# Two small round trips through DRAM are moved from SyncE's queue to GpSimd's, and the first groups are reordered

## The reference

```
x = x + rg_lru(layernorm(x))                      # a gated recurrence with two projections
x = x + xattn(ctx, latents=layernorm(x))          # 8 heads of 128; keys and values: 722 context rows + 100 latents
x = x + moe(layernorm(x))                         # 8 experts, each token to the one with the highest gate
xattn: q = ln(lat) @ Wq + bq;  k, v = split(concat(ln(ctx), ln(lat)) @ Wkv + bkv)
       out = softmax(q k^T / sqrt(128)) v @ Wo + bo
```

## Time and profile before

| | |
|---|---|
| median of 3 timed runs | 1144.46 us (1142.28 to 1147.23) |
| profiled execution | 1131.91 us, span 1130.1 us |
| TensorE busy | 1024.0 us, 91% |
| VectorE busy | 816.0 us, 72% |
| ScalarE busy | 586.3 us, 52% |
| GpSimd busy | 123.7 us, 11% |
| mean granted TensorE clock | 0.956 of 2.4 GHz |

### The profile page before, as it was taken

How to read it: one execution, slowest core, us unless ns; L and a number is a source line. 1 busy time by engine, 2 the same in 40 slices (tenths; PEclk the granted TensorE clock), 3 DMA queues, 4 the chain that set the end, 5 groups by cost and what they waited for, 6 DMA issues and landing times.

```text
span 1130.1 us, 14844 instructions
## 1 busy us (share of the span) xinstructions
PE 1024.0 (91%) x5274; PEld 935.4 (83%) x5275; DVE 816.0 (72%) x1083; ACT 586.3 (52%) x766; POOL 123.7 (11%) x100
## 2 busy tenths in 40 slices
PE   8999998587969979889799799986998999999997
PEld 6979988587969969889699699986885888888876
DVE  6987458596868768678688676667576893966991
ACT  4437566145526425445264363556354784856871
POOL 4534001000000000000000000000011121211230
PEclk9999999798999989989999899997998999999999
DMA  9344794441631524516317131466934992975970
GB/s 282 107 153 158 253 302 119 115 138 37 162 85 35 165 76 125 144 37 161 85 39 217 21 81 37 139 238 210 317 120 155 320 355 98 341 271 171 356 264 21
DMA packets 119934, 183.89 MB, mean 163 GB/s; under 512 B 39024, under 2 KB 62064, under 8 KB 119874
## 3 DMA queue, kind: packets, MB, share of 16 engines
q1 hardware_dynamic: 118194, 178.55, 50.6%
q0 software_dynamic: 1680, 4.54, 1.2%
HBM read 146.94 MB, written 37.11 MB: 163 GB/s over the span
## 4 chain that ended last, share of the span: by engine, by line
PE 55%; DMA 24%; DVE 8%; ACT 6%; issue 3%; SPq 2%; POOL 0%; DVEq 0%; POOLq 0%; ACTq 0%
PE bank L579 16%; PE bank L580 15%; PE bank L581 15%; DMA scr_inverse<-iv 9%; DMA scr_rows<-mvr 5%; DMA raw<-in_ctx 5%; DMA inv<-scr_inverse 3%; ACT xn_h L1443 2%; PE bank L1320 2%; DVE str__65 L1702 1%; PE bank L1140 1%; PE bank L1047 1%; PE bank L1049 1%; PE bank L1048 1%; ACT pa L1458 1%
## 5 line engine op out<-in xcount | busy, mean ns | idle before, releaser
L579 PE MATMUL bank<-ph,xn_h 128*128 128x400 f32 x384 | 148.2, 386 | 13.6 <-DVE zf L1985 9.6
L1720 DVE TENSOR_TENSOR wsl<-stage,wsh 128x2048 fp32r<-128x2048 f32 x63 | 143.7, 2291 | 23.2 <-ACT wsh L1508 18.5
L580 PE MATMUL bank<-pl,xn_h 128*128 128x400 f32 x384 | 139.2, 362 | 0.0
L581 PE MATMUL bank<-ph,xn_l 128*128 128x400 f32 x384 | 137.7, 359 | 0.0
L579 PE MATMUL bank<-qt_h,xt_h 128*128 128x400 f32 x384 | 133.8, 348 | 0.0
L580 PE MATMUL bank<-qt_l,xt_h 128*128 128x400 f32 x384 | 131.9, 343 | 0.0
L581 PE MATMUL bank<-qt_h,xt_l 128*128 128x400 f32 x384 | 131.6, 343 | 0.0
L1508 ACT CAST wsh<-stage 128x2048 fp32r<-128x2048 f32 x63 | 120.4, 1918 | 11.1 <-PE bank L581 7.9
L1481 ACT ACTIVATE zf<-zf,gbm 128x400 f32<-128x400 f32 x64 | 40.0, 628 | 157.6 <-DVE zf L1985 157.6
L1458 ACT ACTIVATE pa<-bank,rsr 128x400 f32<-128x400 f32 x96 | 56.4, 591 | 73.5 <-PE bank L581 73.3
L579 PEld LDWEIGHTS bank<-ph,xn_h 128*128 128x128 f32 x384 | 78.2, 204 | 18.2 <-DVE zf L1985 11.6
(11 more groups left out here) (273 smaller groups left out, 2354.1 us busy)
## 6 DMA issues: line engine op xcount, KB each, us to landing
stage<-in_W SPq DMA_DIRECT2D x63, 1024.0 KB, 6.4
scr_q<-st SPq DMA_DIRECT2D x16, 800.0 KB, 6.5
qf<-scr_q SPq DMA_DIRECT2D x16, 800.0 KB, 11.5
scr_z<-zf SPq DMA_DIRECT2D x16, 800.0 KB, 5.0
zr<-scr_z SPq DMA_DIRECT2D x16, 800.0 KB, 6.1
rt<-in_ctxT SPq DMA_DIRECT2D x7, 1444.0 KB, 19.0
raw<-in_ctx SPq DMA_DIRECT2D x8, 768.0 KB, 6.2
raw<-in_ctx SPq DMA_DIRECT2D x8, 512.0 KB
```

Source lines behind the costliest of these rows:

```text
L579: pe.matmul(dest, lh, rh, start=start and k == 0, stop=False)
L580: pe.matmul(dest, lh, rl, start=False, stop=False)
L581: last = pe.matmul(dest, ll, rh, start=False, stop=stop and k == n - 1)
L1720: return dve.tensor_tensor(dst, src, high.bitcast(F32), ALU.subtract)
```

## The change

The functions `store_mean`, `load_mean` and `spread_inverse` leave SyncE's program and go to GpSimd's, with all their places in it. GpSimd issues them and waits for them itself, in the order mean 1, rows_std 1, and then for each b: inverse 2b, mean b + 2, `rows_std` of b + 2, inverse 2b + 1. Both kinds of store count on one semaphore, `s_kept`. The inverse is stored tokens first, (t h), so that the 4 heads of a token are one run of 16 bytes; `weighted` reads it accordingly. In the first groups VectorE takes the statistics of sequence 1 before the maxima of group 0, centres half of the keys before the weights of group 0, and makes the inverse of group 0 before the other half; ScalarE starts on the rows before the first scores and waits for the query stores later; TensorE turns and spreads the maxima of group 0 one chunk of scores earlier. In the last group `spread_sums` moves into the middle of the first piece of the context.

```diff
@@ semaphores
-    s_row, s_rt, s_ltin, s_ltout = sem("s_row"), sem("s_rt"), sem("s_ltin"), sem("s_ltout")
+    s_mrow, s_rt, s_ltin, s_ltout = sem("s_mrow"), sem("s_rt"), sem("s_ltin"), sem("s_ltout")
...
@@ SyncE
-            store_mean(1)
-            load_mean(1)
...
             for b in range(B - 1):
-                spread_inverse(2 * b)
                 sp.wait_ge(s_s, KC * (2 * b + 2))
...
                     load_keys(b + 2)
-                    store_mean(b + 2)
-                    sp.wait_ge(s_nr, (b + 1) * 2)
-                    load_mean(b + 2)
                 write_z(b, 0)
...
-                spread_inverse(2 * b + 1)
                 write_z(b, 1)
...
-            spread_inverse(NU - 2)
...
-            spread_inverse(NU - 1)
@@ GpSimd
-            for b in range(1, B):
-                rows_std(b)
...
+            def store_mean(b):
+                pool.wait_ge(s_mvr, b + 1)
+                pool.dma_start(d_row[b].rearrange("(c p) -> p c", p=P), mvs[b % 2][:, :, 0], allow_slow_non_contiguous=True
+                               ).then_inc(s_kept, 16)
+
+            def load_mean(b):
+                pool.wait_ge(s_kept, kept("mean", b))
+                pool.wait_ge(s_nr, (b - 1) * 2)
+                pool.dma_start(mrow[:], bc(d_row[b, 0:MEDIA], MEDIA)).then_inc(s_mrow, 16)
+
+            def spread_inverse(u):
+                b, g = divmod(u, 2)
+                pool.wait_ge(s_inv, u + 1)
+                pool.dma_start(d_iv[u].rearrange("(t h) -> t h", h=GH), iv[0:T, b, g * GH:(g + 1) * GH]).then_inc(s_kept, 16)
+                pool.wait_ge(s_kept, kept("inverse", u))
+                pool.wait_ge(s_zn, ND * u)
+                pool.dma_start(inv[:], bc(d_iv[u], GR)).then_inc(s_ivl, 16)
+
+            store_mean(1)
+            load_mean(1)
+            rows_std(1)
+            for b in range(B - 1):
+                spread_inverse(2 * b)
+                if b + 2 < B:
+                    store_mean(b + 2)
+                    load_mean(b + 2)
+                    rows_std(b + 2)
+                spread_inverse(2 * b + 1)
+            spread_inverse(NU - 2)
+            spread_inverse(NU - 1)
@@ TensorE
-                    if u == 1 and c == 1:
+                    if u == 1 and c == 0:
                         turn_maxima(0)
-                    elif u == 1 and c == 3:
+                    elif u == 1 and c == 2:
                         spread_maxima(0)
...
-            context(NU - 1, 0)
-            spread_sums(NU - 1)
+            context(NU - 1, 0, lambda: spread_sums(NU - 1))
@@ ScalarE
-            act.wait_ge(s_cout, 16 * 2)
-            for k in range(5):
-                act.wait_ge(s_qout[k], 16 * sum(stage_of(i, j)[0] == k for i in range(2) for j in range(HEADS)))
-
+            act.wait_ge(s_qout[4], stores_of(4))
+            rows_high(0, 0)
             for c in range(KC):
...
-                if c in (0, 2, 4):
-                    rows_high(0, c // 2)
+                if c == 1:
+                    rows_high(0, 1)
+                elif c == 3:
+                    act.wait_ge(s_cout, 16 * 2)
+                    for k in range(4):
+                        act.wait_ge(s_qout[k], stores_of(k))
+                    rows_high(0, 2)
@@ VectorE
-                                  inv[:].rearrange("p (h t) -> p h t", h=GH), ALU.mult).then_inc(s_zn, 1)
+                                  inv[:].rearrange("p (t h) -> p h t", h=GH), ALU.mult).then_inc(s_zn, 1)
...
+            for k in range(2):
+                dve.wait_ge(s_qout[k], stores_of(k))
             for part in range(3):
                 rows_low(0, part)
+            rows_stats(1, 0)
             first_maximum(0)
+            rows_stats(1, 1)
             last_maximum(0)
...
                     shifts(0)
-                    rows_stats(1, 0)
                     for part in range(NP):
                         shift(0, part)
-                    rows_stats(1, 1)
+                    keys_centred(1, 0)
+                    weights(0)
                     first_maximum(1)
-                    weights(0)
                     last_maximum(1)
+                    inverse(0)
+                    keys_centred(1, 1)
                     queries(1, 0)
-                    for half in range(2):
-                        keys_centred(1, half)
-                    inverse(0)
```

More of the change, by code:

```diff
@@ L294, in stage_of, with stores_of @@
         return k, len(earlier)
+    def stores_of(k):
+        return 16 * sum(stage_of(i, j)[0] == k for i in range(2) for j in range(HEADS))
     wq = mem("wq", [P, ND, INNER])
@@ L406, in build @@
     s_x1l, s_x2out = [sem("s_x1l0"), sem("s_x1l1")], [sem("s_x2out0"), sem("s_x2out1")]
-    s_zb, s_zn, s_zbeta, s_ivd, s_ivl = sem("s_zb"), sem("s_zn"), sem("s_zbeta"), sem("s_ivd"), sem("s_ivl")
+    s_zb, s_zn, s_zbeta, s_kept, s_ivl = sem("s_zb"), sem("s_zn"), sem("s_zbeta"), sem("s_kept"), sem("s_ivl")
     s_xnh, s_xnl, s_s, s_ev, s_a6, s_mx, s_mt, s_dg = (sem(n) for n in (
@@ L672, in load_keys @@
                 sp.dma_start(rt[:], a["ctxT"][b].rearrange("(c p) m -> p c m", p=P)).then_inc(s_rt, 16)
[L674 to L681, removed]
             def load_latent_keys(b):
@@ L773, in load_weights @@
                     sp.dma_start(stage[j % 4][:], w_src(which, e, f)).then_inc(s_w[j % 4], 16)
[L775 to L782, removed]
             sp.wait_ge(s_rawz, 2)
@@ L933, in router_std, with kept @@
                 pool.sem_inc(s_rsx, 1)
-            for b in range(1, B):
-                rows_std(b)
+            kept_in_order = [("mean", 1)]
+            for b in range(B - 1):
+                kept_in_order += [("inverse", 2 * b)] + [("mean", b + 2)] * (b + 2 < B) + [("inverse", 2 * b + 1)]
+            kept_in_order += [("inverse", NU - 2), ("inverse", NU - 1)]
+            def kept(what, n):
+                return 16 * (kept_in_order.index((what, n)) + 1)
+            def store_mean(b):
[16 more added lines that the diff above has]
+            rows_std(1)
+            for b in range(B - 1):
+                spread_inverse(2 * b)
[6 more added lines that the diff above has]
+            spread_inverse(NU - 1)
             for b in range(NT):
@@ L1586, in _ @@
                 if u == 1:
-                    for c in range(4):
+                    for c in range(3):
                         evacuate(1, c)
@@ L1592, in _ @@
                     exponentials(0, 2)
+                    evacuate(1, 3)
                     evacuate(1, 4)
                     weights_high(0, 1)
+                    weights_high(0, 2)
                     evacuate(1, 5)
-                    weights_high(0, 2)
                     evacuate(1, 6)
@@ L1864, in keys_centred @@
                 if half == 0:
-                    dve.wait_ge(s_rt, 32 * b)
+                    dve.wait_ge(s_rt, 16 * b)
+                    dve.wait_ge(s_mrow, 16 * b)
                 dve.tensor_tensor(x, x, mrow[:].unsqueeze(1).broadcast_to([P, 2, MEDIA]), ALU.subtract).then_inc(s_nr, 1)
```

## The result

The changed kernel takes 1090.01 us (median of 4 runs, 1087.55 to 1090.84) beside 1143.76 us (1142.28 to 1147.23) of the kernel before: a ratio of 0.9522, interval 0.9495 to 0.9549. A second measurement on another chip gave 0.9551, 0.9514 to 0.9588. The forecast was 1103.5 in a range of 1082 to 1140.

The account below looks back on a forecast made before the run. TensorE was taken to be held by small transfers, chiefly the even groups' inverse stores delaying `dg`. Even groups 34, first groups 3, last group 4 sum to 41 us: 1131.9 to 1091, the median to 1103.5, range 1082 to 1140.

Parts of the forecast that it names:

- the carry: From profiled execution (1131.9 us) to timed median (1144.46): the forecast gain in us was carried over unchanged.
- Leaving SyncE's queue, and the runs of four: Inverse store: SyncE's queue no longer delays it; 100 runs for 400 make a quiet store 3.3 us, bounds 2.6 to 6.2.
- Through GpSimd's queue: Mean and inverse transfers: each takes 1.0 us more by GpSimd than by SyncE, bounds 0 and 2.4.
- Even groups: Six even groups: TensorE resumes after `dg` 5.2 us earlier, plus 0.5 us of clock; 34 us in all.
- The clock: TensorE in even groups: 0.5 us back in each of six from the clock's fall after the wait for `dg`.
- Odd groups: Odd groups: inverse round trip 9.3 us for 9.8, TensorE's wait of 1 us stays or shrinks; gain 0.
- The first groups: Start of attention, new order: inverse of group 0 earlier, 3 us gained; bounds a loss of 4, a gain of 7.
- The last group: Final group: sums moved into mid-context and a shorter inverse trip cut TensorE's 13.92 us wait; 4 us, between 2 and 6.
- The stepped read: VectorE's multiply reading `inv` with a 16-byte step: costed at nothing; at double, 0.6 us a group.
- B: Rival: even inverse stores stay 11.3 us from any queue, because all issuers share the DMA engines; 1149.5 us, chance 0.09.
- D: Rival, slower: GpSimd's issue of the 768-run mean store takes 15 us, plus 8.9 to land; 1173 us, chance 0.13.
- C, the queries next: Rival: in even groups the queries' load keeps 11.5 us and becomes the next limit; 1121 us, chance 0.14.

Follow-up runs that it names:

- runs alone: Kernel before with only the inverse stored in 16-byte runs and read accordingly, everything still issued by SyncE: 1063.11 us, ratio 0.9358.
- runs, z write up: Kernel before with the inverse in 16-byte runs and the z write placed between the mean's store and load, all by SyncE: 1072.22 us, ratio 0.9453.
- runs and order: Kernel before with the inverse in 16-byte runs and the change's order of first and last groups, all by SyncE: 1062.38 us, ratio 0.937.
- runs, order, z write up: Kernel before with 16-byte inverse runs, the change's group order and the z write between mean store and load, by SyncE: 1071.16 us, ratio 0.9443.
- the change with the old order: Changed kernel with the first groups ordered as before, the last group as changed: 1090.99 us, ratio 0.9603.
- the mean's return to SyncE: Changed kernel with the mean's store and load back in SyncE, the inverse still issued by GpSimd in 16-byte runs: 1070.31 us, ratio 0.9452.
- both in runs: Kernel before with inverse and mean both stored in runs, all by SyncE, first groups in the old order: 1062.41 us, ratio 0.9392.

## Why the prediction was right, and where it was not

The traces give the change in three stretches: from the end of the query projection to the inverse store of group 2, the five pairs from there to that of group 12, and from there to the end of the last wait for `zf`. Each number is a difference of two starts in a timeline, in us. Traces on one chip have the same letter; the first trace of the change and that of before come without one.

| | chip | to group 2 | five pairs | last |
|---|---|---|---|---|
| before | | 134.0 | 374.6 | 114.9 |
| before, again | A | 134.9 | 374.8 | 114.9 |
| runs alone | A | 125.4 | 325.6 | 107.7 |
| runs, z write up | B | 125.7 | 334.0 | 107.7 |
| runs and order | B | 120.5 | 328.0 | 107.7 |
| runs, order, z write up | B | 123.7 | 332.4 | 107.7 |
| the change (runs, order, queue) | | 129.3 | 342.4 | 107.6 |
| the change, again | B | 129.1 | 337.8 | 107.5 |
| the change with the old order | A | 134.2 | 339.0 | 107.5 |

The change twice differs by 4.6 us in the five pairs, so smaller differences there say nothing.

Where a pair gains is seen from the inverse store that opens it (the one with nothing ahead). Means over the five pairs, us from that store to the start of

| | centring | maxima's transposes | spread of `dg` | next pair |
|---|---|---|---|---|
| before | 37.6 | 42.0 | 52.6 | 74.9 |
| runs alone | 34.6 | 38.9 | 45.0 | 65.1 |
| the change | 37.5 | 41.8 | 48.2 | 68.5 |

**The total.** Between the two profiled executions the gain is 1131.91 - 1090.84 = 41.1 us, for a sum of 41. VectorE's wait of 1.95 us for `raw` is gone from this pair, as forecast. Between the timed medians it is 53.8 us. The whole miss of 13.5 us is thus in the carry: "I carry the difference in us over to that median". The 12.5 us by which the kernel before's profiled execution lay below its timed ones is not there in the kernel after. That the sum itself is met to 0.1 us is luck, for its terms miss in both directions. The first stretch, which holds one even group and the new order, was to give 5.7 + 3 = 8.7 us and gives 4.7; the five pairs were to give 28.5 and give 32.2; the last 4, and it is 7.3; and the changed kernel's trace begins the attention stage 3.1 us later (152.69 for 149.59), which no term has. Traces of the other kernels begin it anywhere from 149.1 to 152.1. By the timed medians the sum is 13 us short.

**Leaving SyncE's queue, and the runs of four.** The prediction never split its 34 us: the runs were to take 2.5 us off a quiet store (5.8 to 3.3), and the rest of the even store's fall from 11.7 to 4.3 us was to come from leaving the queue. The runs of the kernels say the opposite: the runs alone by SyncE give 74 us (1136.87 to 1063.11), the queue and order without them cost 22 (1159.35), and of the gain of the runs the move gives back 19.5, of which 8.8 are the z write that now runs beside the mean store. The mis-sized term is the store: quiet 1.3 us, not 3.3, and outside the bounds of 2.6 to 6.2. The nearest row, `rec` with 768 runs, was a store of nearly eight times as many runs; I took its time and not its time for a run.

**Through GpSimd's queue.** 1.0 us a transfer, bounds 0 and 2.4: with runs of 16 bytes and nothing beside it, it is 1.98 for 1.3, 0.7 more; with 400 runs of 4 bytes 7.8 for 5.8, 2.0 more, though with key loads beside it for the second half; the first mean store 9.9 and 9.4 in the two traces of the change, for 9.0 by SyncE in the same order, 0.4 to 0.9 more. In the even groups the mean store is 12.0 for a forecast of 9.9, since the z write stands beside it now: by SyncE, with the z write put there, it is 10.1 to 12.2, for 8.8 to 11.2 without. The step "VectorE is no later there than now" held all the same, since the mean was ready 3.6 us earlier in the pair (20.6 us behind the store that opens it for 24.2) and not 2.0: the centring starts 37.1 us behind that store for 37.8. VectorE's idling for the mean row grows from 3.75 to 6.61 us because VectorE comes to it earlier, not because the row is later.

**Even groups.** Per pair (374.6 - 342.4) / 5 = 6.4 us for 5.7. Of these 4.4 come by the spread of `dg` and 2.0 after it, in the odd group. In the pair that the prediction worked out, `dg` was to be spread 47.6 us behind the opening store (331.2 - 283.60), and is at 47.3 (329.32 - 282.01). The trip of the inverse is about 5.9 us (2.08 and a load that lands 3.8 us after its issue), for 9.3, but it ends 3.5 us before VectorE comes to `zf`, so the mis-sized store didn't move the spread of `dg`. "What is late next is VectorE with the mean row ahead of it" was right, and the place was wrong: TensorE meets it at the transposes of the maxima, 3.68 us, two pieces ahead of `dg`, which I had down for some 2 us and which is 0.27. The prediction followed VectorE's list through the maxima and never asked when TensorE wants them, though the wait of 9.9 us for them was in the trace of before.

**The clock.** I counted 0.5 us in each of six groups. TensorE is busy 1015.9 us for 1024.0, 8 us less for the same 5274 matmuls, at a mean granted clock of 0.963 for 0.956. On one chip, from the kernel before to the runs alone (1019.4 at 0.958, 1006.4 at 0.975), the span falls by 62.1 us, of which 13.0 are busy time and 49.1 idle time. In both pairs the idle time that goes brings about a quarter of itself again in busy time.

**Odd groups.** At nothing, and with transfers 2.4 us longer a loss. The wait of 0.7 to 1.3 us for `dg` is gone altogether, as TensorE is busy through the whole first window: the spread comes 10.7 us behind the quiet inverse store, for 11.8 to 12.4 before. That is 1.4 us a pair that the sum had at nothing. The loss that the prediction priced for longer transfers came in the kernel without the runs, and it is larger there than its 2.3 us a group.

**The first groups.** 3 us; the order moves the first stretch by 4.9 us in two comparisons across chips (125.4 to 120.5 by SyncE, 134.2 to 129.3 by GpSimd) and by 2.0 us in one on the same chip (125.7 to 123.7), so it gains something of the forecast's size there. In the five pairs it makes between 1.6 us less and 3.4 more, within what the change differs from itself, and the timed ratios show nothing. TensorE's 9.49 us wait is 8.70, not 6.5, and a new one of 3.92 us for the maxima of group 0 (185.53 in the timeline) is the price of the row statistics ahead of them. From the inverse store of group 0 to its load it is 5.1 us there (209.59 to 214.65), for 2.0 in group 3, and for 1.3 of the same store by SyncE with runs and order. On one chip the move to GpSimd costs 8.6 us in the first stretch (120.5 to 129.1), nearly as much as the 9.8 in the five pairs together (328.0 to 337.8).

**The last group.** 4 us; it is 7.3, the wait 8.78 for 13.92. Neither the order nor the queue has a part in it: the runs alone give 107.7 for the stretch.

**The stepped read.** Costed at nothing, 0.6 us a group at double. It is 0.29 us for each of the four pieces, 18 us of VectorE in all, and the changed kernel doesn't pay it as far as the ratios can tell (0.9545 without the step, 0.9522 and 0.9551 with it), as VectorE waits for the mean row anyhow; only in the last stretch does its trace show a gain, 105.7 for 107.6 us. In the kernel with runs alone it wasn't tried.

**A reading that was wrong.** The sentence that a store beside other traffic takes twice as long as a quiet one names, which has quiet stores only (5.79 and 6.18 us); the long one, 11.7 us, is in the earlier trace rows.

**The rivals.** B's price (no gain in even groups) was wrong, as the inverse store there does shrink; its mechanism is right and was shown by the mean's return to SyncE. D, slower through GpSimd, was given 0.13. Its sign came without the runs (1.02), but not by its mechanism: GpSimd issues the mean store of 768 runs in 0.86 to 1.11 us, not 15, and the store takes 12, not 22. C, the queries next, didn't come: their median landing is 7.1 us for 11.5, with 8.4 for the runs alone, where they wait in the same queue as ever.

## What to carry to other kernels

When a small transfer is on the path, look first at how many runs it has and how long they are, and only then at whose queue it is in: the layout gave 74 us here and the move took back 19.5. Take the two apart before judging a change that has both. When a queue is freed, ask what its other transfers will now run beside: 8.8 of the 19.5 us were a write that had moved up beside a small store on the path. After removing a wait, go through the other engine's program in order and find the first thing that it wants from the late one, not the thing it waited for until now.

## What the runs showed of the hardware that I had not expected

- A store of 1.6 KB from 100 partitions with nothing beside it is 5.79 us in 400 runs of 4 bytes and 1.3 us in 100 runs of 16 bytes, by SyncE. The mean store of 3 KB with nothing beside it is 8.7 us in 768 runs of 4 bytes (191.91 in the kernel before) and 1.4 us in 128 runs of 24 bytes (192.23 with both in runs). With other traffic beside it the second is 5.1 to 6.0 us in the last five groups that have one.
- VectorE's float32 multiply of 400 elements takes 574 ns with the row read straight and 861 with a step of 16 bytes; the subtraction of 1444 takes 1.66 us, and 3.05 in two instructions with a step of 24 bytes.
- GpSimd's power of 128x6 numbers, 1.36 us in the changed kernel, took 8.25 us once in seven times in one trace. VectorE was busy without a gap beside it, but also beside five of the others (1.5 to 1.9 us), so the cause is open.
- The z write beside the mean store keeps the DMA engines busy for longer than the data explain: a share of 0.82 at 171 GB/s in the changed kernel's first window, and 0.79 at 172 with the z write moved up by SyncE (275.43 to 308), against 0.60 at 152 with the runs alone (277.44 to 309) and 0.57 at 134 before. So it goes with the z write's place and not with the issuing engine; with the mean store in runs of 24 bytes beside the z write it is 0.67 at 195 (283.48 to 316).
